# One-core masked attention layer on Trainium2: output transposes, score matmuls, a copy and a tile load put at other places in the queues

## The reference, cut to what matters

```python
# x: (16, 1024, 512), adj: (1024, 1024) of 0 and 1, 8 heads of 64
h = jnp.maximum(_layernorm(x), 0.0)
q = (h @ Wq + bq).reshape(b, n, 8, 64)      # k and v likewise
scores = jnp.einsum('bihd,bjhd->bhij', q, k) / 8.0
scores = scores + jnp.where(adj == 0, -1e9, 0.0)[None, None]
weights = jax.nn.softmax(scores, axis=-1)
out = jnp.einsum('bhij,bjhd->bihd', weights, v)
return x + out.reshape(b, n, 512)
```

## Time and profile before

| | |
|---|---|
| median of 3 runs | 4067.93 us (4066.05 to 4071.46) |
| the profiled execution | 4066.34 us, its span 4064.5 us |
| granted TensorE clock | 0.999 of full speed on the mean |
| PE busy | 4017.7 us, 99% |
| ACT, DVE, POOL busy | 76%, 75%, 34% |
| DMA engines | 27% |

### The profile page before, as it was taken

One profiled execution on the slowest core, in us unless ns is written; L12 is line 12 of the kernel. 1 busy time (PEld: TensorE's weight loads), 2 busy tenths in 40 slices (PEclk: granted clock), 3 DMA queues, 4 the chain that ended last, 5 costly groups with the idle time before them and its releaser, 6 DMA issues. The chain is left out here.

```text
span 4064.5 us, 64393 instructions
## 1 busy us (share of the span) xinstructions
PE 4017.7 (99%) x22016; PEld 3277.6 (81%) x22016; DVE 3064.8 (75%) x5128; ACT 3077.6 (76%) x5514; POOL 1401.6 (34%) x1409
## 2 busy tenths in 40 slices
PE   7999999999999999999999999999999999999998
PEld 6888888888888888888888888888888888888886
DVE  6877867777777777777777687776877868768686
ACT  5877868778687786877868688686886868868687
POOL 4333333333333333333333333333333333333322
PEclk9999999999999999999999999999999999999999
DMA  5232223222223232222222232222322313223121
GB/s 183 69 93 63 85 59 84 86 65 83 70 72 86 66 85 80 62 83 80 74 81 64 78 92 61 81 79 64 93 66 77 85 59 91 83 59 98 38 73 47
DMA packets 239955, 314.83 MB, mean 77 GB/s; under 512 B 16401, under 2 KB 147473, under 8 KB 231057
## 3 DMA queue, kind: packets, MB, share of 16 engines
q1 hardware_dynamic: 239632, 310.71, 26.8%
HBM read 172.23 MB, written 37.75 MB: 52 GB/s over the span
## 5 line engine op out<-in xcount | busy, mean ns | idle before, releaser
L830 DVE TENSOR_TENSOR pT<-T,pT 128x512 fp32r<-128x512 f32 x2048 | 1390.7, 688 | 750.2 <-ACT pT L665 733.4
L665 ACT CAST pT<-T 128x512 fp32r<-128x512 f32 x2048 | 1186.1, 591 | 656.4 <-PE T L546 575.4
L824 DVE CUSTOM_DVE_ANT_0 S<-S,mask 128x1024 f32<-128x1024 f32 x1024 | 1252.1, 1223 | 3.1 <-PE S L535 3.1
L546 PE MATMUL T<-ident,probs 128*128 128x128 f32 x8192 | 1231.8, 273 | 1.0 <-ACT probs L673 0.6
L546 PEld LDWEIGHTS T<-ident,probs 128*128 128x128 f32 x8192 | 1006.6, 140 | 277.7 <-DVE pT L830 41.4
L673 ACT ACTIVATE probs<-S,negmax 128x1024 f32<-128x1024 f32 x1024 | 1151.5, 1124 | 8.4 <-DVE negmax L824 5.2
L565 PE MATMUL O<-pT,vs 128*64 128x512 f32 x2048 | 964.5, 471 | 0.2 <-DVE pT L830 0.2
L558 PE MATMUL O<-pT,vs 128*128 128x512 f32 x2048 | 816.1, 398 | 0.0
L504 PE MATMUL misc<-hT,wqk 128*128 128x512 f32 x3036 | 787.4, 395 | 7.7 <-ACT y L656 7.7
L504 PEld LDWEIGHTS misc<-hT,wqk 128*128 128x128 f32 x3036 | 556.9, 188 | 160.7 <-issue 42.9
L409 POOL TENSOR_TENSOR outs<-outs,oT 64x512 f32<-64x512 f32 x256 | 336.1, 1313 | 562.4 <-DMA outs<-oT 556.2
(11 more groups left out here) (70 smaller groups left out, 3587.5 us busy)
## 6 DMA issues: line engine op xcount, KB each, us to landing
wqk<-wqk_split SPq DMA_DIRECT2D x63, 1024.0 KB, 7.1
xln<-in_x SPq DMA_DIRECT2D x240, 256.0 KB, 2.7
outs<-in_x SPq DMA_DIRECT2D x66, 512.0 KB, 4.8
kA<-kA SPq DMA_DIRECT2D x128, 256.0 KB, 3.2
kB<-kB SPq DMA_DIRECT2D x128, 256.0 KB, 3.8
outs<-oT SPq DMA_DIRECT2D x256, 128.0 KB, 3.1
out<-outs SPq DMA_DIRECT2D x64, 512.0 KB, 4.4
probs<-in_adj SPq DMA_DIRECT2D x4, 1024.0 KB, 5.0
```

The lines of the kernel that those rows point to most:

```text
L546: mm = pe.transpose(T[:, u % 2, i * P:(i + 1) * P], probs[:, (GB * g + i) % RING, j * P:(j + 1) * P], ident[:])
L665: act.copy(pT[:, u % PT, 0, :], T[:, u % 2, :]).then_inc(p_hi, 1)
L824: dve.tensor_tensor_reduce(S[:, s % 2, :], S[:, s % 2, :], mask[:, s % NB, :], 1.0, 3.0e38, ALU.add, ALU.min, negmax[:, s % RING:s % RING ...
L830: dve.tensor_tensor(pT[:, u % PT, 1, :], T[:, u % 2, :], pT[:, u % PT, 0, :].bitcast(F32), ALU.subtract).then_inc(p_lo, 1)
```

## The change

It has these parts:

- In units 34 and 66 `turn_out` stands right behind `turn_probs`, ahead of the scores and of `contract_hi` (`OUT_DIRECT`). Units 2, 98 and 10 of each 32 stay as they are.
- In units 2, 34, 66 and 98 ACT does `copy_y` ahead of the exponential (`COPY_FIRST`).
- Of the scores that start in units 0, 4, 36, 68, 100, 122, 124 and 126, the first 512 columns are made in that unit and the other 512 in the next one, ahead of its `fill` (`HALVED`). The `shift` of that block moves to the odd unit too.
- On SP, `load_xln` stands ahead of `copy_k` in a unit that has both, and the second half of `copy_k` is written in unit 16 of the 32, not 15.

```diff
--- before.py
+++ after.py
@@ -71,9 +71,10 @@
 STATS_SLOTS = (5, 7, 11, 13, 37, 39, 43, 45)
 STATS_AT = {s: t for t, s in enumerate(STATS_SLOTS)}
 
-COPY_K_AT, STORE_AT, RES_AT, WQK_AT = (8, 15), 19, 24, (21, 21, 28, 21)
+COPY_K_AT, STORE_AT, RES_AT, WQK_AT = (8, 16), 19, 24, (21, 21, 28, 21)
 
 OUT_AT, FINISH_AT = (2, 10), (3, 17)
+OUT_DIRECT, COPY_FIRST = (34, 66), (2, 34, 66, 98)
 PER = UNITS // PAIRS
 
 
@@ -82,6 +83,7 @@
 V_EARLY = len(V_SLOTS)
 V_AT = {s: (1, j) for j, s in enumerate(V_SLOTS)} | {j: (0, V_EARLY + j) for j in range(NB - V_EARLY)}
 V_SPLIT_AT = {s + 1: v for s, v in V_AT.items() if s + 1 < UNITS} | {0: (0, V_EARLY - 1)}
+HALVED = (4, 36, 68, 100, 122, 124, 126, 0)
 XLN = 2
 XLN_USES = [len(range(r, NB, XLN)) for r in range(XLN)]
 
@@ -321,13 +323,13 @@
                         t = STATS_AT[u]
                         sp.wait_ge(bn_done, NB * (b + 1) + t + 1)
                         load_xln(b + 1, (t + XLN) % NB)
-                    for half in range(2):
-                        if v == COPY_K_AT[half] and not (last and p == PAIRS - 1):
-                            copy_k(b, p + 1, half)
                     if u in HT_AT and HT_AT[u] + XLN < NB and not last:
                         t = HT_AT[u]
                         sp.wait_ge(h_turned, NB * (b + 1) + t + 1)
                         load_xln(b + 1, t + XLN)
+                    for half in range(2):
+                        if v == COPY_K_AT[half] and not (last and p == PAIRS - 1):
+                            copy_k(b, p + 1, half)
                     if v == WQK_AT[p] and not (last and p >= PAIRS - 2):
 
                         sp.wait_ge(qk_mm, 4 * (PAIRS * b + p + 1) + 4)
@@ -518,22 +520,24 @@
                                    start=n == 0, stop=n == len(parts) - 1)
                 mm.then_inc(v_mm, 1)
 
-            def score(b, s):
+            def score(b, s, halves=(0, 1)):
 
                 n = SBLOCKS * b + s
                 q, k = qk_buffers(s // 16, (s // 8) % 2)
                 i = s % NB
                 pair = PAIRS * b + s // 16
-                pe.wait_ge(q_low, 4 * pair + 3 + (s // 8) % 2)
-                pe.wait_ge(k_copied, 64 * (pair + 1))
-                if some(n - 1):
-                    pe.wait_ge(exped, n - 1)
-                for half in range(2):
+                if 0 in halves:
+                    pe.wait_ge(q_low, 4 * pair + 3 + (s // 8) % 2)
+                    pe.wait_ge(k_copied, 64 * (pair + 1))
+                    if some(n - 1):
+                        pe.wait_ge(exped, n - 1)
+                for half in halves:
                     cols = slice(half * HALF, (half + 1) * HALF)
                     dst = S[:, s % 2, cols]
                     pe.matmul(dst, q[:, i * P:(i + 1) * P], k[:, 0, cols], start=True, stop=False)
                     mm = pe.matmul(dst, q[:, i * P:(i + 1) * P], k[:, 1, cols], start=False, stop=True)
-                mm.then_inc(scored, 1)
+                if 1 in halves:
+                    mm.then_inc(scored, 1)
 
             def turn_probs(b, u):
 
@@ -576,10 +580,11 @@
 
             def score_ahead(b, u, last):
                 s = u // 2 + LEAD
-                if u % 2 == 0 and s < SBLOCKS:
-                    score(b, s)
-                if u % 2 == 0 and s >= SBLOCKS and not last:
-                    score(b + 1, s - SBLOCKS)
+                halves = (u % 2,) if u // 2 * 2 in HALVED else (0, 1) if u % 2 == 0 else ()
+                if halves and s < SBLOCKS:
+                    score(b, s, halves)
+                if halves and s >= SBLOCKS and not last:
+                    score(b + 1, s - SBLOCKS, halves)
 
             def fill(b, u, last):
                 if u in V_AT and not (last and u >= V_FROM):
@@ -611,11 +616,13 @@
 
 
                         turn_probs(b, u)
+                        if u in OUT_DIRECT:
+                            turn_out(b, u // PER - 1, OUT_AT.index(u % PER), before(b, u, True, last))
                         score_ahead(b, u, last)
                         contract_hi(b, u - LAG)
                         if u in OUT_AT and not first:
                             turn_out(b - 1, PAIRS - 1, OUT_AT.index(u), before(b, u, True, last))
-                        if u >= PER and u % PER in OUT_AT:
+                        if u >= PER and u % PER in OUT_AT and u not in OUT_DIRECT:
                             turn_out(b, u // PER - 1, OUT_AT.index(u % PER), before(b, u, True, last))
                         contract_lo(b, u - LAG)
                         continue
@@ -749,14 +756,18 @@
                     if u > 1 and u % NB == 1:
                         copy_out(b, u // NB - 1)
                     probs_hi(b, u)
+                    if u in COPY_FIRST and u in OUT_AT and not first:
+                        copy_y(b - 1, PAIRS - 1, OUT_AT.index(u))
+                    if u in COPY_FIRST and u >= PER and u % PER in OUT_AT:
+                        copy_y(b, u // PER - 1, OUT_AT.index(u % PER))
                     s = u // 2 + LEAD - 1
                     if u % 2 == 0 and s < SBLOCKS:
                         exponential(b, s)
                     if u % 2 == 0 and s >= SBLOCKS and not last:
                         exponential(b + 1, s - SBLOCKS)
-                    if u in OUT_AT and not first:
+                    if u not in COPY_FIRST and u in OUT_AT and not first:
                         copy_y(b - 1, PAIRS - 1, OUT_AT.index(u))
-                    if u >= PER and u % PER in OUT_AT:
+                    if u not in COPY_FIRST and u >= PER and u % PER in OUT_AT:
                         copy_y(b, u // PER - 1, OUT_AT.index(u % PER))
                     if u in V_SPLIT_AT and not (last and u > V_FROM):
                         nxt, j = V_SPLIT_AT[u]
@@ -888,9 +899,10 @@
                         h_low(b + 1, HT_AT[u - 1])
                     probs_low(b, u)
                     s = u // 2 + LEAD
-                    if u % 2 == 0 and s < SBLOCKS:
+                    due = u % 2 == (1 if u // 2 * 2 in HALVED else 0)
+                    if due and s < SBLOCKS:
                         shift(b, s)
-                    if u % 2 == 0 and s >= SBLOCKS and not last:
+                    if due and s >= SBLOCKS and not last:
                         shift(b + 1, s - SBLOCKS)
                     if u in V_AT and not (last and u >= V_FROM):
                         bias_v(b + V_AT[u][0], V_AT[u][1])
```

## The result

The changed kernel takes 4016.35 us on the median (4014.92 to 4017.08), the kernel before 4069.04 us beside it: a ratio of 0.987, 95% interval 0.9853 to 0.9888. Forecast were 4017 us and a range of 4008 to 4030. The profiled execution took 4017.08 us with a span of 4015.3 us, 49.2 us less than the span before; the sum of the prediction was 49.3 us.

The account below looks back on a forecast made before the run. The prediction took TensorE, 99% busy, as the bound, with stalls hidden in its busy time. Gains of 12.6 + 10.1 + 18.8 + 7.8 = 49.3 us from 4066.3 us gave 4017 us, range 4008 to 4030 us.

Parts of the forecast that it names:

- (a): Units 35, 67, 99: a q or k projection waits for ACT's copy of the turned output; 47 x 0.40 = 18.8 us.
- (b): Units 5, 37, 69, 101: the second projection waits until ACT has evacuated the first; 63 x 0.20 = 12.6 us.
- (c): Units 125, 127, 1: a projection of V directly behind another waits for DVE; 46 x 0.22 = 10.1 us.
- (d): Unit 85: transposes of tile 3 of x wait for POOL, and POOL for the tile's load; 7.8 us.
- R1: Rival: the odd-unit projections' waits for ACT or DVE move to the next projection instead of going; 4040 us, chance 0.07.
- Costs at nothing: DVE's `shift` one unit later for divided scores: costed at nothing; without cover, 1.22 us in each of 125 places.
- R3: Rival: ACT becomes the bound in units 2 and 98, its copy waiting for transposes; 4105 us, chance 0.04.
- R4: Rival: distances of starts are how the profile draws matmuls, not stalls; nothing won, 4066 us, chance 0.03.
- The weight load: A wait exposing one 128-column load costs 0.107 us, not 0.07; over 156 places 6 us more gained, 4011 us.

Follow-up runs that it names:

- the test with four moved: Changed kernel, but in units 122, 124, 126 and 0 all four score matmuls, not two, moved to the odd unit: 4027.92 us.
- the kernel with twelve copies: Changed kernel with twelve small unused copies, each waited for, between ACT's copy and exponential in units 2, 34, 66 and 98: 4199.74 us.

## Why the prediction was right

The forecast and its mechanism held, step by step. Taken unit by unit from the traces of the two kernels (from the start of one unit's transposes to the next, summed over the batches), part (a) took 19.2 us off its units, (b) 13.0, (c) 9.6 and (d) 8.1, where the prediction had 18.8, 12.6, 10.1 and 7.8. For (c) the first batch's units 0 and 1 are left out, since the start of the kernel alters them by 1 us.

That 49.2 us of the spans meet the sum of 49.3 so closely is in part luck. The profiled execution before, 4066.34 us, was one of the fast ones (its runs beside the result lie between 4066.05 and 4071.46), and by the medians the gain is 52.7 us, 3 us more than the sum. Kernels that keep the old order on SP spread by 5.4 to 8.4 us in their runs, those with the new order by 1.2 to 3.8 us. What varies goes with that order, so most likely it is the wait of (d), and the 3 us more are its own; no trace of a slower execution of the kernel before is there to show it.

- **(b) and (c)**, 12.6 + 10.1 = 22.7 us: alone they gave a ratio of 0.9942, 23.6 us of 4069, with an interval from 17.5 to 30.1 us. Two score matmuls were cover enough on both sides, and the test with four moved shows that both sides need it. With this R1 falls: no wait moved to ACT or DVE.
- **(a)**, 18.8 us: taking the copy's place back cost 19.4 us. The prediction described the two edits together and left open which of them counts; it is the copy alone. That eight transposes in a row cost what two groups of four do, which no row before showed, stands in the timeline after: 2112.22, 2112.66 and 2113.01 are 0.44 and 0.35 us apart, and the next matmul comes at 2113.33: 1.11 us in all, which is eight steps of 0.11 and one of 0.23. Standing there they took away a wait of ACT, and no one's time.
- **(d)**, 7.8 us: the load order alone gave a ratio of 0.9976, 9.8 us of 4069, with an interval from 6.1 to 13.8 us that holds it; its trace has 8.1 us less in unit 85. The size of this wait varies from batch to batch and from run to run, as its line shows (10.4, 11.2 and 12.0 us of idle time in the kernel before and the two that keep the old order), so it is the least sure of the terms.
- **Costs at nothing**: `shift` one unit later made PE wait nowhere in the eight places of the change (its waits for DVE's low part are 167 before and 167 with the divided scores alone); with a ninth place, unit 76, there are 15 new ones. The cover that the prediction named, DVE's idle time, was the right thing to check, but it has to be checked for each place.
- **R3** was the sharpest rival, and its point of decision was right: the exponential ends 1.62 us ahead of the score, 1.38 us of it can be used, and what goes beyond is paid in full. **R4** falls with the time itself.

- **The weight load.** The estimate of 4011 us rests on the 0.107 us that the Trainium skill ("TensorE: Matmul & The Clock Gate", LDWEIGHTS (loading the stationary operand)) gives for 128 columns. The medians can't tell it from the 0.07 us of the rows, since their 52.7 us lie between the 49.3 and the 55 us of the two. The traces speak for the rows: the six matmuls behind a wait are shown with 1.62 us before and 1.55 after, and the units of (a), (b) and (c) gained 41.8 us together, against 41 by the rows and, an estimate, 47 by the page. The loads themselves are longer in the trace than by the page, 0.19 us for one of a projection.

## What to carry to other kernels

Where an engine is shown 99% busy, read the distances between starts in the timeline and compare places of the same kind: the stalls here were mostly 0.2 to 0.4 us each, mostly invisible as idle time of PE, repeated 171 times, and 1.2% of the kernel. A shared buffer whose hand-over takes a fixed time wants that much other work ahead of each new use; where one use has work to spare and the next has none, divide a block between the two rather than move it. When reordering a queue, look at what stands behind on that queue until the next consumer, place by place: 1.3 us more cost next to nothing on ACT here, 4 us cost 2.3 of them and 0.6 more by the clock. A later `shift` on DVE was free in eight units and cost more than it won in the ninth.

## What had not been expected of the hardware

In the kernel with twelve copies PE stood for 2.41 us in unit 4 of batch 8; after that the granted clock was at the lower of its levels, 0.50, and 1.55 us of matmuls took 2.71. After the 1.86 us of unit 36 of that batch the six matmuls took their 1.55 us. The mean granted clock of that kernel was 0.991, against 0.998 after the change.

The length of the idle time doesn't decide it alone. In that trace the clock fell behind 15 of 30 idle times of 2.4 us (13 of 15 in unit 4, but 2 of 15 in unit 100, where they are as long), behind 3 of 32 of 1.9 us in units 36 and 68, and behind one of 3.8 us. What else decides it stays open here. So a stall of PE that is made longer can cost more than its length, and by how much can't be read from one place. The kernel before, at 0.999, shows nothing of it: its clock is at the lower level only once, 59 us from the start, and at the end.
